# First cross attention of a two-layer model: queries by pairs of heads, in slots written out

## The reference, cut to what matters

```python
def _L0_xattn_ref(x, cond, Wq, bq, Wkv, bkv, Wp, bp):   # x: 8 x 256 x 256, cond: 512 rows of context
    H, hd = (16, 16)
    q = (x @ Wq + bq).reshape(1, B * N, H, hd)
    kv = (cond @ Wkv + bkv).reshape(1, -1, 2, H, hd)
    k, v = (kv[:, :, 0], kv[:, :, 1])
    q = jnp.transpose(q * 0.25, (0, 2, 1, 3))
    q = _fq_sym(q, axis=-1)          # rounded to 127 steps of each head's largest value
    k = _fq_sym(k, axis=-1)
    v = _fq_sym(v, axis=2)
    attn = jnp.einsum('bhqd,bhkd->bhqk', q, k)
    attn = jax.nn.softmax(attn, axis=-1)
    attn = _fq_unsigned(attn, axis=-1)   # rounded to 255 steps of each row's largest value
    out = jnp.einsum('bhqk,bhkd->bhqd', attn, v)
    return out @ Wp + bp                 # and x = layernorm(x + this)
```

## Time and profile before

| | |
|---|---|
| median of 3 runs | 3485.99 us (3485.69 to 3489.45) |
| the profiled execution's own time | 3490.39 us |
| its span in the trace | 3488.6 us |
| busy: PE, DVE, ACT, POOL | 79%, 53%, 45%, 35% of the span |
| TensorE clock granted, mean over the span | 0.833 of full speed |

### The profile page before, as it was taken

How to read it: one execution, slowest core, us unless ns; L and a number is a source line. 1 busy time by engine, 2 the same in 40 slices (tenths; PEclk the granted TensorE clock), 3 DMA queues, 4 the chain that set the end, 5 groups by cost and what they waited for, 6 DMA issues and landing times. The chain is left out here.

```text
span 3488.6 us, 49109 instructions
## 1 busy us (share of the span) xinstructions
PE 2766.1 (79%) x13661; PEld 1696.1 (49%) x13663; DVE 1854.6 (53%) x4142; ACT 1553.7 (45%) x3112; POOL 1204.1 (35%) x1132
## 2 busy tenths in 40 slices
PE   5799999879999975887887937887477525988884
PEld 2477777646777753444444513333344212455552
DVE  4676666666666656767773156774322510222334
ACT  3555555455555543767771115665155200123331
POOL 1477777437777740000000021000100063144443
PEclk8999999989999985555557957998679755899997
DMA  1122111012122106500000000000000051377875
GB/s 61 46 55 51 34 51 37 7 49 55 27 53 55 37 12 208 170 1 0 1 1 29 0 17 1 1 1 1 21 1 0 1 179 69 69 163 169 180 172 124
DMA packets 127079, 192.70 MB, mean 55 GB/s; under 512 B 17552, under 2 KB 88208, under 8 KB 125584
## 3 DMA queue, kind: packets, MB, share of 16 engines
q1 hardware_dynamic: 83696, 134.71, 13.7%
q0 software_dynamic: 23616, 33.24, 5.4%
q10 hardware_dynamic: 19584, 22.57, 2.4%
HBM read 123.23 MB, written 67.25 MB: 55 GB/s over the span
## 5 line engine op out<-in xcount | busy, mean ns | idle before, releaser
L228 DVE SCALAR_TENSOR_TENSOR h_pre<-h_px,h_par,h_pre 128x510 f32<-128x510 f32 (+2 forms) x384 | 286.5, 746 | 270.6 <-ACT h_pre L689 250.7
L843 POOL TENSOR_TENSOR norm_rstd<-norm_mv,mhalf 128x4 f32<-128x4 f32 x24 | 28.2, 1177 | 1023.3 <-DVE norm_mv L826 1023.3
L652 PE MATMUL h_po<-h_wo,h_h 128*128 128x256 f32 x1024 | 329.3, 412 | 0.0
L2906 POOL DMA_INDIRECT moe_sums<-ex_y,ex_sidx x132 | 204.8, 1552 | 321.1 <-DVE ex_y L3074 302.9
L574 POOL TENSOR_SCALAR h_decay<-h_cumb,h_sel 128x256 f32<-128x256 f32 x256 | 292.0, 1141 | 25.4 <-DMA h_cumb<-cum_rows 25.4
L585 POOL TENSOR_TENSOR h_mix<-h_decay,cb 128x768 f32<-128x768 f32 x128 | 232.9, 1820 | 166.3 <-ACT h_decay L675 166.3
L616 PE MATMUL h_px<-x_cols,h_w 128*128 128x512 f32 x512 | 254.4, 620 | 25.6 <-DMA h_d<-d_skip 25.6
L1256 ACT ACTIVATE xq_ex<-xq_ps,xq_nmax,xq_qs 128x512 f32<-128x512 f32 x256 | 199.4, 779 | 113.6 <-DVE xq_nmax L1324 113.0
L621 PE MATMUL h_pz<-x_cols,h_w 128*128 128x512 f32 x512 | 242.4, 596 | 5.7 <-DVE h_gate L742 5.6
L1322 DVE TENSOR_REDUCE xq_top<-xq_ps 128x1 f32<-128x512 f32 x256 | 176.3, 689 | 83.5 <-PE xq_ps L1169 81.7
L701 ACT ACTIVATE h_xt<-h_pxt,h_sel 128x128 f32<-128x128 f32 x512 | 146.4, 369 | 152.2 <-PE h_pxt L640 152.2
(11 more groups left out here) (390 smaller groups left out, 6004.6 us busy)
## 6 DMA issues: line engine op xcount, KB each, us to landing
h_cumb<-cum_rows SPq DMA_DIRECT2D x32, 1024.0 KB, 8.6
moe_tiles<-blank SPq DMA_DIRECT2D x4, 6642.0 KB, 44.1
ex_w<-moe_w SPq DMA_DIRECT2D x64, 352.0 KB
ex_xg<-moe_tiles ACTq DMA_DIRECT2D x136, 162.0 KB
ex_wd<-moe_wd SPq DMA_DIRECT2D x64, 176.0 KB
h_w<-w_xg SPq DMA_DIRECT2D x8, 1024.0 KB, 10.4
moe_sums<-blank SPq DMA_DIRECT2D x2, 2176.0 KB, 26.7
h_wo<-w_out SPq DMA_DIRECT2D x8, 512.0 KB, 10.3
```

The source lines that it names most:

```text
L228: ins = dve.scalar_tensor_tensor(out=out[:, :, back:S], in0=src[:, :, 0:S - back], scalar=par[:, at + CK - 1 - back:at + CK - back], in1=o ...
L652: pe.matmul(po[t // TPB][:, t % TPB, :], hh[j % 2][:, t * P:(t + 1) * P], w_out[s.pg][:, j, :], start=(j == 0 and t % TPB == 0), stop=(j = ...
L2906: pool.indirect_dma_start(out=r.sums[i % 2][:, :], out_offset=bass.IndirectOffsetOnAxis(ap=sidx[i][:, 0:1], axis=0), in_=y[i % 2][:], in_o ...
```

## The change

An item becomes a pair of heads, `ND` = 16 of them for a batch. Its scores fill two banks, so `ps` takes four banks instead of two; `pa` and `prT` hold both heads' transposes in one tile; `ex` has 3 buffers of a pair in place of 4 of a head. `po` has one buffer in place of two, and one bank `pt` serves the query product, both kinds of transposes and the output product, which had two banks. Maximum, rounding and keep are one instruction for a pair; score, bias and exponential stay one for each head.

A batch has 16 slots. `due(turn, m, at)` says whose step is due: `at` is the step's place counted from the start of the turn in which its batch's query is made. In slot j PE issues the turn of pair j-2, the score of j+1 and the mix of j-3; ACT the keep of j-2 and the exponential of j; DVE the maximum of j and the rounding of j-1. Behind them come the batch's own steps: query in slot 0, quantise in slots 1 to 5, normalise of the batch before in slot 3, its oturn in 4, its out in 6, its add in 8, qturn and qkeep in 9 and 11. All 8 batches are written out; there is no loop.

The query product reads `r.xT` directly and fetch is gone. The quarter of the scale and the bias come in one instruction; the last rounding writes `qparts` directly, and POOL makes the other two copies. POOL also adds the output's bias to the rows, ahead of add.

```diff
-        xcol = sb("xcol", [P, KE, S])
+        XH2 = XH // 2
+        ND = TPB * XH2
...
+        ex = [sb(f"ex{i}", [P, 2, M]) for i in range(3)]
+        pr = [sb(f"pr{i}", [P, 2, M], BF16) for i in range(2)]
+        prT = [sb(f"prT{i}", [P, 2, M], BF16) for i in range(2)]
...
-        pq = psum("pq", [P, TPB, E])
-        pt = psum("pt", [P, 8 * P], BF16)
-        ps = [psum(f"ps{i}", [P, M]) for i in range(2)]
-        pa = [psum(f"pa{i}", [P, 8 * P], BF16) for i in range(2)]
-        po = [psum(f"po{i}", [P, TPB, E]) for i in range(2)]
+        pt = psum("pt", [P, TPB, E])
+        ps = [psum(f"ps{i}", [P, 2, M]) for i in range(2)]
+        pa = [psum(f"pa{i}", [P, 2, M], BF16) for i in range(2)]
+        po = psum("po", [P, TPB, E])
...
-        NORM, OTURN, OKEEP, OUT, ADD = 1, 4, 4, (6, 7), 8
-        FETCH, QUERY, QUANT, QTURN, QKEEP = 8, (10, 12), 13, (21, 23), (21, 23)
-        QUANTS = 6
-
-        def head(cur, nxt, m):
...
+        SLOTS = ND
+        QUERY, QUANT, QTURN = 0, (1, 2, 3, 4, 5), (9, 11)
+        SCORE, TOP, EXP, ROUNDED, TURN, KEEP, MIX = 15, 16, 16, 17, 18, 18, 19
+        NORM, OTURN, OUT, ADD = 35, 36, 38, 40
+
+        def due(turn, m, at):
+
+            s = turn + 1 - at // SLOTS
+            return s if at % SLOTS == m and 0 <= s < B else None
+
+        def slots():
+            return [(turn, m) for turn in range(-1, B + 1) for m in range(SLOTS)]
...
             pool.memset(qparts[:], 0.0).then_inc(cleared, 1)
+            pool.wait_ge(cleared, 1)
+
+            def repeat(s):
+                pool.wait_ge(rounded_q, s + 1)
+                for c in range(1, 3):
+                    ins = pool.tensor_copy(qparts[:, :, c * XD:(c + 1) * XD], qparts[:, :, 0:XD])
+                ins.then_inc(quantised, 1)
+
+            def base(s):
+                for u in range(TPB):
+                    ins = pool.tensor_tensor(r.x[:, s * TPB + u, :], r.x[:, s * TPB + u, :], bp[:], ALU.add)
+                ins.then_inc(based, 1)
+
+            for s in range(B):
+                repeat(s)
+                base(s)
...
+                after(pe, qkept, s * TPB)
+                for u in range(TPB):
+                    for k in range(KE):
+                        mm = pe.matmul(pt[:, u, :], r.xT[:, k, s * S + u * P:s * S + (u + 1) * P], wq[:, k, :],
+                                       start=(k == 0), stop=(k == KE - 1))
+                mm.then_inc(queried, 1)
...
+            def score(s, d):
+                u, h2 = divmod(d, XH2)
+                if h2 == 0:
+                    pe.wait_ge(qkept, s * TPB + u + 1)
+
+                after(pe, expd, s * ND + d - 1)
+                for par in range(2):
+                    lo = 64 * par
+                    mm = pe.matmul(ps[d % 2][:, par, :], qT[s % 2][u][lo:lo + 64, h2, :], keysT[lo:lo + 64, h2, :],
+                                   start=True, stop=True)
+                mm.then_inc(scored, 1)
...
+            def turn_pr(s, d):
+                pe.wait_ge(rounded, s * ND + d + 1)
+                after(pe, pkept, s * ND + d - 1)
+                for par in range(2):
+                    for c in range(KM):
+                        mm = pe.transpose(pa[d % 2][:, par, c * P:(c + 1) * P], pr[d % 2][:, par, c * P:(c + 1) * P], r.identb[:])
                 mm.then_inc(pturned, 1)
...
+            def mix(s, d):
+                u, h2 = divmod(d, XH2)
+                pe.wait_ge(pkept, s * ND + d + 1)
+                if d == 0:
+
+                    after(pe, scaled, s)
+                for par in range(2):
+                    h = 2 * h2 + par
+                    for c in range(KM):
+                        mm = pe.matmul(po[:, u, h * XD:(h + 1) * XD], prT[d % 2][:, par, c * P:(c + 1) * P],
+                                       vals[:, c, h * XD:(h + 1) * XD], start=(c == 0), stop=(c == KM - 1))
                 mm.then_inc(mixed, 1)
...
+            for turn, m in slots():
+                for d in range(ND):
+                    if (s := due(turn, m, TURN + d)) is not None:
+                        turn_pr(s, d)
+                for d in range(ND):
+                    if (s := due(turn, m, SCORE + d)) is not None:
+                        score(s, d)
+                for d in range(ND):
+                    if (s := due(turn, m, MIX + d)) is not None:
+                        mix(s, d)
+                if (s := due(turn, m, QUERY)) is not None:
+                    query(s)
+                if (s := due(turn, m, OTURN)) is not None:
+                    oturn(s)
+                if (s := due(turn, m, OUT)) is not None:
+                    out(s)
+                for u in range(TPB):
+                    if (s := due(turn, m, QTURN[u])) is not None:
+                        qturn(s, u)
 
         @block.scalar
         def _(act):
-            for sm in (fetched, qkept, expd, pkept, okept):
-                act.drain().then_inc(sm, LEAD)
...
-            def fetch(s):
-                act.wait_ge(queried, LEAD + s.b)
-                act.activation(xcol[:], r.xT[:, :, bass.ds(s.b * S, S)], ACT.Copy).then_inc(fetched, 1)
...
+            def exp(s, d):
+                act.wait_ge(topped, s * ND + d + 1)
+
+                after(act, rounded, s * ND + d - 2)
+                for par in range(2):
+                    at = 2 * d + par
+                    ins = act.activation(ex[(s * ND + d) % 3][:, par, :], ps[d % 2][:, par, :], ACT.Exp, bias=nmax[s % 2][:, at:at + 1],
+                                         scale=qs[s % 2][:, at:at + 1], accum_out=tot[s % 2][:, at:at + 1])
+                ins.then_inc(expd, 1)
...
+            for turn, m in slots():
+                for d in range(ND):
+                    if (s := due(turn, m, KEEP + d)) is not None:
+                        keep(s, d)
+                for d in range(ND):
+                    if (s := due(turn, m, EXP + d)) is not None:
+                        exp(s, d)
+                if (s := due(turn, m, OTURN)) is not None:
+                    okeep(s)
+                for u in range(TPB):
+                    if (s := due(turn, m, QTURN[u])) is not None:
+                        qkeep(s, u)
 
...
+                    dve.scalar_tensor_tensor(out=q[:], in0=pt[:], scalar=0.25, in1=bq[:], op0=ALU.mult, op1=ALU.add).then_inc(biased, 1)
...
-                elif part == 4:
-                    dve.tensor_scalar(q[:], q[:], ROUND, ROUND, ALU.add, ALU.subtract)
...
+                    dve.tensor_scalar(qparts[:, :, 0:XD], qh, ROUND, ROUND, ALU.add, ALU.subtract).then_inc(rounded_q, 1)
...
+            def maxed(s, d):
+                at = 2 * d
+                dve.wait_ge(scored, s * ND + d + 1)
+                dve.tensor_reduce(top[:, at:at + 2], ps[d % 2][:], AX.X, ALU.max, negate=True)
+                dve.drain()
+                for one in range(at, at + 2):
+                    ins = dve.tensor_scalar(nmax[s % 2][:, one:one + 1], top[:, one:one + 1], qs[s % 2][:, one:one + 1], LN255, ALU.mult, ALU.add)
+                ins.then_inc(topped, 1)
...
+                dve.wait_ge(based, s + 1)
+                rows = r.x[:, s * TPB:(s + 1) * TPB, :]
+                dve.tensor_tensor(rows, pt[:], rows, ALU.add).then_inc(added, 1)
...
+            for turn, m in slots():
+                for d in range(ND):
+                    if (s := due(turn, m, TOP + d)) is not None:
+                        maxed(s, d)
+                for d in range(ND):
+                    if (s := due(turn, m, ROUNDED + d)) is not None:
+                        rnd(s, d)
+                if (s := due(turn, m, NORM)) is not None:
+                    normalise(s)
+                if (s := due(turn, m, ADD)) is not None:
+                    add(s)
+                for part in range(5):
+                    if (s := due(turn, m, QUANT[part])) is not None:
+                        quantise(s, part)
```

More of the change, by code:

```diff
@@ L1198, in oturn @@
                 mm.then_inc(oturned, 1)
-            def out(s, u):
-                pe.wait_ge(okept, LEAD + s.b + 1)
-                for k in range(KE):
-                    mm = pe.matmul(pq[:, u, :], oT[:, u, k * P:(k + 1) * P], wp[:, k, :],
-                                   start=(k == 0), stop=(k == KE - 1))
-                if u == TPB - 1:
-                    mm.then_inc(outed, 1)
-            def slot(cur, nxt, m):
-                for ahead, part in ((4, score), (0, mix), (2, turn)):
-                    if m + ahead >= 0 and head(cur, nxt, m + ahead):
-                        part(*head(cur, nxt, m + ahead))
@@ L1213, in body @@
-            def body(prev, cur, nxt):
-                for m in range(TH):
-                    if prev and m == OTURN:
-                        oturn(prev, False)
-                    if prev and m in OUT:
-                        out(prev, OUT.index(m))
-                    if nxt and m in QUERY:
-                        query(nxt, QUERY.index(m))
-                    if nxt and m in QTURN:
-                        qturn(nxt, QTURN.index(m))
```

(20 more changed lines are left out.)

201 lines of the change are left out of this document (54 added, 147 removed).

## The result

| | before | after |
|---|---|---|
| median of 4 runs, same chip | 3487.72 us (3485.69 to 3490.55) | **3377.61 us** (3365.58 to 3380.53) |
| ratio, 95% interval | | 0.9677 (0.9651 to 0.9703) |
| the profiled execution's own time, its span | 3490.39, 3488.6 | 3380.53, 3378.8 |
| the stage (below), us | 499.4 | 397.6 |
| middle batch, us | 61.57 | 47.7 |

On the other chips the kernel before took 3404 to 3409 us (medians; its last stage took 667 us in the execution profiled there, 741 here). A second run of the changed kernel there gave 3305.53 against 3406.84 for the kernel before, 0.9693 (0.9673 to 0.9712): 101 us. The one profiled execution of the kernel before there took 3412.88.

A forecast was written before the change was run, and what follows sets the result against it. Score ring (1.29 us a head), ACT and DVE were taken as level within some 4%. Gains of 65.2 (six middle batches), 8.9 and 4.3, together 78.4, turn 3490.4 into 3412.0, as a median 3408 us; range 3382 to 3442.

The forecast's parts named there:

- 16 pairs: Undisturbed pairs of a batch: 2.50 us each, 40.0 a batch, ACT the bound; bounds 2.45 and 2.58 a pair.
- query, beyond a pair: Slot 0: the query's fp32 matmuls, about 3.7 us less PE's slack, cost 3.2; bounds 1.6 and 3.7.
- out: Slot 6: the output's fp32 matmuls, about 3.7 us less PE's slack, cost 3.2; bounds 1.6 and 3.7.
- slots 1 to 5: Quantise and normalise on DVE, okeep, and the first mix's wait for `po`: 2.45 us a batch; bounds 0.5 and 4.6.
- qturn and qkeep: PE's transposes run beside ACT's exponential; qkeep costs ACT 0.91 us, twice: 1.8 a batch.
- rival B: Clock rises behind fp32 work: query and out at 2.4 GHz, 1.6 us less for each of 15: 3384; chance 0.12.
- the jumps: Loop's two jumps back, 3.0 us each, go when batches are written out; already counted in the 61.57 a batch.
- rival C: POOL's copies and adds block DVE on the path: 2.6 x 8 = 21 us, total 3429; chance 0.09.
- the edges: First and last pair's longer chain, repaid by the lost fetch and bias add: taken as 0, within 2 us.
- Nothing gives way: Kernel before: ring, ACT and DVE within some 4% of each other, so any step beside the items stops all.
- the ring: Kernel before: score through maximum, bias, exponential and read to the score two heads on, 2.58 us, 1.29 a head.
- 20.3 of a batch are its own steps at nearly full price: Kernel before: beyond 41.3 us of heads, 20.3 a batch is its own steps plus two jumps back.

The follow-up runs named there:

- Experiment 5: Both kernels run again, plus the changed kernel with POOL's query copies and bias adds back on DVE: that one's stage 398.3 us, total 3305.44 against 3305.53.
- 13: Changed kernel with PE's own batch steps ahead of the turn, score and mix of their slot: stage 409.8 us against 397.6, total 3319.66.
- 9: Changed kernel with query and out spread over slots, and normalise issued ahead of its slot's rounding: stage 369.4 us, total 3278.18, ratio 0.9616.
- experiment 6: Changed kernel with each of the eight fp32 products of query and out in its own slot: stage 374.9 us, total 3281.22, ratio 0.9636.
- Experiment 2: Kernel before, written out, with three score buffers of single heads instead of two, normalise one place earlier: stage 491.1 us, total 3410.63, ratio 1.0005.
- 4: Changed kernel with the mixes between a pair's two scores, so these do not run side by side: stage 421.5 us, total 3330.49.
- 1: Kernel before with its eight batches written out, nothing else changed: stage 492.6 us against 499.4, total 3407.63, ratio 1.0015.
- 12: Kernel before, written out, single heads, with DVE relieved, PE's batch steps behind their place and three score buffers: stage 442.3 us, total 3359.85, ratio 0.9862.
- experiment 8: Changed kernel with the output product computed twice in the same slot: stage 412.5 us against 397.6 and 399.8, total 3319.08.

## Why the prediction was right and wrong

The direction held, and so did the mechanism of the changed kernel: ACT is its bound, and its batch steps find slack. Two terms of the sum were mis-sized. A late middle batch by the prediction's terms, predicted and measured:

| term | predicted | measured (first run, second run) |
|---|---|---|
| 16 pairs | 40.0 | 38.6 (2.415 each) |
| query, beyond a pair | 3.2 | 3.38, 2.35 |
| out | 3.2 | 1.86, 2.92 |
| slots 1 to 5 | 2.45 | 2.11 |
| qturn and qkeep | 1.8 | 1.80 |
| batch | 50.7 | 47.8, 47.8 (mean of the six: 47.7, 48.0) |

**The pair: the step that failed first.** The prediction worked out 2.45 and then took 2.50, as an allowance for small waits. There are none once there is slack: 2.415 in every undisturbed pair, under the stated lower bound too, since 0.66 + 0.09 stood where I had taken 0.68 + 0.09 and 0.90 for 0.91. That is 0.085 x 128 = 10.9 us. The chain that feeds ACT is as forecast: two scores together 0.61, maximum 1.22, as the groups by line of after say, answering to the earlier trace rows:

```profile
L1306 DVE TENSOR_REDUCE xq_top<-xq_ps 128x2 f32<-128x1024 f32 x128 | 156.5, 1222 | 17.7 <-PE xq_ps L1175 14.1
```

**Query and out: the second.** I priced both wholly at the low clock, 3.2 each, and gave rival B, both at the full clock, 0.12. Neither was right. PE in the first run, around the query and around out, in one batch:

```profile
1588.98 0.61 PE L1175 MATMUL xq_ps<-x_keysT,xq_qT 64*128 64x512 bf16 x2 [0.55 <-ACT xq_ex L1253]
...
1589.76 3.76 PE L1148 MATMUL xq_pt<-x_wq,x_cols 128*128 128x256 f32 x8
1593.31 1.06 PE L1184 MATMUL xq_pa<-identb,xq_pr 128*128 128x128 bf16 x8
...
1609.32 3.06 PE L1214 MATMUL xq_pt<-x_wp,xq_oT 128*128 128x256 f32 x8
1612.21 0.61 PE L1184 MATMUL xq_pa<-identb,xq_pr 128*128 128x128 bf16 x8
```

The first row is a pair's two scores, and the 0.55 is PE's wait of an undisturbed pair. Out's eight records took 3.06, then eight transposes 0.61 instead of 1.06. The windows on both (PEclk is the first number behind the busy times) say why:

```profile
1591.00:1594.00 3.00, 3.00 (x13) 2.28 (x13) 1.41 (x4) 0.36 (x2) 0.00 (x0) 0.50 0.00 0
1610.00:1613.00 3.00, 3.00 (x18) 2.24 (x16) 2.27 (x5) 1.27 (x5) 0.79 (x1) 0.75 0.00 0
1613.00:1616.00 3.00, 1.44 (x28) 0.97 (x26) 2.12 (x4) 3.00 (x6) 0.00 (x0) 1.00 0.00 0
```

Query runs at 0.50 (1.2 GHz). Within out PE has been busy without a pause, and the granted clock goes to 1.00 (2.4 GHz): half of that window, all of the next. The rise comes with the fifth of the eight records (their starts are 0.43 apart, then 0.22), so over half of the burst is paid at the low clock, and what follows behind it is cheap. In the second run of the same kernel it is the other way round:

```profile
1594.27 3.14 PE L1148 MATMUL xq_pt<-x_wq,x_cols 128*128 128x256 f32 x8
1597.24 0.61 PE L1184 MATMUL xq_pa<-identb,xq_pr 128*128 128x128 bf16 x8
...
1612.81 3.76 PE L1214 MATMUL xq_pt<-x_wp,xq_oT 128*128 128x256 f32 x8
1616.36 0.98 PE L1184 MATMUL xq_pa<-identb,xq_pr 128*128 128x128 bf16 x8
```

There the query rises and out doesn't, and their sum is 5.27 instead of 5.24. Experiment 5 has a third split (query 3.1, out 1.1, 1.1 more elsewhere) and again batches of 47.8. So mostly one rise a batch, at one burst or the other: 1.2 us off the forecast for each of 7, 8 us. It is no rule of the kernel. Batch 1 of the second run has no rise at either burst and takes 48.9, batch 2 a late one and 48.0, which is most of the 2.2 us by which that stage is longer; and the batches of 13 alternate between 50.8 and 48.2. Why late batches come out equal at 47.8 in three executions is not shown.

**Slots 1 to 5** were near: 2.11 for 2.45. The wait for `po` behind normalise is there as the prediction followed it (PE's timeline, slot 3), and 9 shows that its place could be mended:

```profile
1506.31 0.36 PE L1196 MATMUL xq_po<-x_vals,xq_prT 128*128 128x16 bf16 x8 [1.71 <-DVE xq_o L1322]
```

**qturn and qkeep** cost 0.90 each as priced, **the jumps** 6.8 for 6.0.

**POOL beside DVE.** In the timeline, POOL's two bias adds of a batch and the roundings on DVE; the second row is the second add by itself:

```profile
1513.48 1.86 POOL L1133 TENSOR_TENSOR x_rows<-x_rows,x_bp 128x256 f32<-128x256 f32 x2
1514.16 1.18 POOL L1133 TENSOR_TENSOR x_rows<-x_rows,x_bp 128x256 f32<-128x256 f32 x1
```

```profile
1513.93 0.82 DVE L1315 TENSOR_SCALAR xq_pr<-xq_ex 128x1024 bf16<-128x1024 f32 x1
...
1516.21 0.69 DVE L1315 TENSOR_SCALAR xq_pr<-xq_ex 128x1024 bf16<-128x1024 f32 x1
```

One rounding a batch is 0.13 longer beside POOL. Nothing waits for it: its transposes stand behind out on PE and start at 1516.70. That is zero, as in the sum, and rival C falls. The Trainium skill ("SBUF — State Buffer", "Who interferes with whom") has the later engine blocked for the whole instruction of the first, where both want the shared ports. The trace agrees, and here it is POOL that pays: an add with nothing of DVE beside it takes 0.73 (1350.41), as the first add does here, while the second, issued 0.23 behind the start of the rounding, takes 1.18. In one batch of experiment 6 DVE is late and that add starts first, at 1513.52; it takes 0.72, and the rounding is the one held, 1.15 for 0.69:

```profile
1513.65 1.15 DVE L1319 TENSOR_SCALAR xq_pr<-xq_ex 128x1024 bf16<-128x1024 f32 x1
```

**The sum.** Against the forecast the stage has 23.4 us more: six middle batches 18.1 (61.57 to 47.7 instead of 50.7), batch 0 2.7, batch 7 2.6. By terms: pairs 10.9, out 9.4, slots 1 to 5 2.4, query -1.3, and some 2 at the edges. With these alone the time would have been 3384, inside the range; the other 7 us came from stages that the change doesn't touch. On the other chips the medians differ by 101.3 us and the stage by 101.1, so by the medians they were absent there. That the time fell outside the range and not just inside it was chance; that it was 23 us off in the stage was not. So the range failed for two reasons: its foot was built from B alone (-24) and not from B's part and the pair's together, and it left no room for what other stages do between programs.

**The picture of before** was half right. "Nothing gives way" held, and its rows were read rightly, but the prediction called the ring the limit at 1.29 and left PE out of the level ones. Experiment 2 shows PE's 1.22 beside ACT and DVE and 1.28 without the ring, and 4 shows that much of the cure lay there: PE's part of a pair went from 2 x 1.22 = 2.44 to 2.41 - 0.55 = 1.86. The prediction also counted "eight fp32 matmuls" where rows 8 show eight records of four matmuls; the price of 3.50 is the same. The step "20.3 of a batch are its own steps at nearly full price" holds for that kernel, but over a fifth of it can be had with single heads: middle batches take 60.4 in 1 and 56.0 in 12 at about the same granted clock (0.55 and 0.53), 52.4 to 53.6 where the clock rises.

## What to carry to other kernels

Where several engines stand within a few per cent of each other, taking one wait away shows nothing (the third buffer: 1.5 us, within the spread of repeats); look for the edit that shortens the engine that every step of the batch uses, put each such step behind the work that others wait for, and try it in pieces over several slots (22.7 us here, slack and clock together). Before two edits are said to help each other, put the granted clock of their batches side by side: here it made most of what looked like help. Price an engine that will be the bound by the starts of its records, without an allowance. Matmuls on 64 rows each, on different halves of the array and issued back to back, are worth checking for in any attention with small heads.

## What the runs showed of the hardware

- Two matmuls of 64 rows of weights and 512 columns, on different rows of the array and issued back to back, take 0.61 us together, one 0.60; with eight small ones between them each costs its own 0.53 (experiment 4). The Trainium skill ("TensorE: Matmul & The Clock Gate", "Part 3: Packing small matmuls — row/col tiling") says that small matmuls on different tiles of the array run concurrently, and the trace agrees.
- ACT hides the accumulator read nearly whole: the next instruction starts 0.09 us behind the read's start, at a recorded duration of 0.19 to 0.39.
- The granted clock of identical code differs between executions in place, and a little in effect: in one run it rose within out's burst in every middle batch, in the next within the query's from batch 2 on, with late batches of 47.8 us in both but a stage 2.2 us longer. It can also differ from batch to batch of one execution: out's burst took 3.76 and 1.97 in turn in 13.
- The records of a burst of fp32 matmuls (128 rows of weights, 256 columns) start 0.43 us apart at the low clock and 0.22 at the full one (experiment 8).
- A POOL add (128x256, f32) takes 0.73 us alone and 1.18 when a rounding of 1024 f32 columns to bf16 runs on DVE as it is issued; issued the other way round, the rounding takes 1.15 for 0.69.
- Eight batches of straight code on three engines showed no stand put down to issue of over 0.45 us, while a taken jump back cost DVE 3.0 us and ACT 2.0.
